# Six slots instead of four for the token tiles of the cluster pass, half of them filled from ScalarE's queue

## What is computed

```python
xn = _layernorm(x, axis=-1)
x = x + attn(xn, w_attn, b_attn, w_proj, b_proj) + ffn(xn, weight, bias, centroids, assignments)
# ffn:
dots = softmax(x @ centroids.T / 0.1, axis=-1)      # 64 clusters
hits = dots > 0.01
query_sel = any(hits, axis=1)                       # per token
cluster_sel = any(hits, axis=0)                     # over ALL tokens
row_sel = cluster_sel[assignments]
out = where(query_sel[:, None] & row_sel[None, :], x @ weight.T + bias, 0)
```

## Time and profile before

| what | us |
|---|---|
| median of 2 timed runs (6993.18 and 7485.42) | 7239.3 |
| the profiled execution, its own time | 7027.4 |
| its span, slowest core (core 1) | 7025.5 |
| spans of the 8 cores | 6952.6 to 7025.5 |
| median span of cores 0 to 3, of cores 4 to 7 | 6993.9, 6974.2 |
| mean granted clock of PE, share of full speed | 0.805 to 0.813 |

### The profile page before, as it was taken

The page is one execution under the profiler, slowest core; times in us unless marked ns, Lnnn a source line. Parts: engine busy times, 40 slices in busy tenths (PEclk is TensorE's granted clock), DMA queues, the critical chain, the costliest instruction groups (busy, mean ns, idle before and its releaser), DMA issues.

```text
span 7025.5 us, 98369 instructions; the slowest of 8 cores (6952.6 to 7025.5 us)
## 1 busy us (share of the span) xinstructions
PE 4684.8 (67%) x20715; PEld 1983.1 (28%) x20715; DVE 1906.3 (27%) x5321; ACT 1679.0 (24%) x3524; POOL 1613.6 (23%) x3133
## 2 busy tenths in 40 slices
PE   2218888888888896666666566355555557777676
PEld 1103333333333332122112111122222223333222
DVE  4421111111111100333333343355333322222222
ACT  4320000000000000222222222133444422222222
POOL 0011111111111111333333333000000034444443
PEclk9999988999988987777777777566555578888888
DMA  3322333323222223443444344211111054443443
GB/s 130 116 90 81 76 80 78 79 78 78 76 79 78 77 68 108 139 137 117 133 139 137 120 130 136 87 46 46 46 46 45 30 155 125 126 124 121 122 124 116
DMA packets 708128, 688.40 MB, mean 98 GB/s; under 512 B 100321, under 2 KB 562145, under 8 KB 701409
## 3 DMA queue, kind: packets, MB, share of 16 engines
q1 hardware_dynamic: 631906, 480.68, 23.8%
q0 software_dynamic: 75648, 201.44, 8.7%
HBM read 606.22 MB, written 75.50 MB: 97 GB/s over the span
## 4 chain that ended last, share of the span: by engine, by line
PE 52%; DVE 12%; ACT 11%; DMA 11%; issue 8%; POOL 3%; SPq 1%; DVEq 1%; ACTq 1%; POOLq 0%
PE p2p L87 27%; PE f5b L87 7%; PE f5a L87 7%; PE qp L87 4%; DMA d3x<-xT_all 4%; ACT a4e L80 4%; DMA qw<-w_attn 3%; ACT p2o L80 3%; POOL d3q L80 2%; DVE statc L80 2%; PE a4po L87 2%; PE a4pt L87 2%; DVE d3r L80 1%; ACT f5t L80 1%; DVE a4o L80 1%
## 5 line engine op out<-in xcount | busy, mean ns | idle before, releaser
L87 PE MATMUL p2p<-xn_fm,p2b 128*128 128x512 bf16 x8192 | 1961.6, 406 | 253.0 <-POOL p2b L80 244.4
L87 PEld LDWEIGHTS p2p<-xn_fm,p2b 128*128 128x128 bf16 x8192 | 840.2, 103 | 1374.0 <-issue 609.7
L87 PE MATMUL f5a<-ofm,f5pb 128*128 128x512 bf16 x2048 | 659.2, 406 | 312.9 <-DVE f5pb L80 312.9
L80 DVE CAST p2b<-p2w 128x128 bf16<-128x128 f32 x1024 | 232.3, 227 | 1972.5 <-PE p2p L87 1700.2
L87 PE MATMUL f5b<-xno,f5fb 128*128 128x512 bf16 x2048 | 651.8, 402 | 94.1 <-DVE f5fb L80 94.1
L87 PE MATMUL qp<-xno,qb 128*128 128x512 bf16 x2048 | 513.9, 410 | 288.6 <-DVE qb L80 229.4
L80 ACT ACTIVATE p2o<-p2p,battn 128x512 bf16<-128x512 f32 x256 | 175.9, 687 | 2052.0 <-PE p2p L87 2034.0
L99 POOL DMA_DIRECT2D f5f<-ffn_wT x1024 | 546.0, 537 | 262.5 <-issue 159.9
L80 POOL CAST p2b<-p2w 128x128 bf16<-128x128 f32 x1024 | 300.8, 294 | 1328.6 <-PE p2p L87 1152.0
L87 PE MATMUL a4po<-a4a,a4e 128*128 128x129 bf16 x2304 | 331.1, 269 | 292.1 <-ACT a4e L80 278.7
L80 ACT ACTIVATE a4e<-a4t 128x128 bf16<-128x128 f32 (+3 forms) x616 | 257.2, 418 | 643.3 <-DVE a4t L80 575.1
(11 more groups left out here) (112 smaller groups left out, 3806.7 us busy)
## 6 DMA issues: line engine op xcount, KB each, us to landing
p2w<-w_attn SPq DMA_DIRECT2D x2048, 64.0 KB, 2.3
d3x<-xT_all SPq DMA_DIRECT2D x512, 256.0 KB, 3.2
f5f<-ffn_wT POOLq DMA_DIRECT2D x1024, 64.0 KB, 2.3
f5p<-w_proj SPq DMA_DIRECT2D x1024, 64.0 KB, 2.1
qw<-w_attn POOLq DMA_DIRECT2D x512, 64.0 KB, 2.4
qw<-w_attn SPq DMA_DIRECT2D x512, 64.0 KB, 2.2
p1x<-x_full SPq DMA_DIRECT2D x16, 1024.0 KB, 5.9
p1x<-x_full POOLq DMA_DIRECT2D x16, 1024.0 KB, 8.0
```

What stands on the lines that cost most here:

```text
L80: instr = getattr(self.e, method)(*args, **kw)
L87: return getattr(self.e, method)(*args, **kw)
```

## The change

Three things change, all in `p3_gen` and its buffers. There are six slots instead of four. Slots 0 to 2 are still filled from SP; slots 3 to 5 are filled by DMAs issued on ACT's queue, with three semaphores of their own (`acq`). The waits in front of a fill are the same as before, but those in front of a fill of slots 3 to 5 now stand on ACT's queue. Even slots (0, 2, 4) are squared by ACT, odd ones (1, 3, 5) by POOL.

```diff
+        acq = [Ch(es, nc, f"acq{i}") for i in range(3)]
...
-                        for s in range(4)]
+                        for s in range(6)]
...
-                                s = (tg * NKC + kc) % 4
+                                s = (tg * NKC + kc) % 6
                                 sqe = AC if s % 2 == 0 else PO
-                                SY.dma(dsq[s], xtt[s][:],
-                                       xT_all[kc * 128:(kc + 1) * 128,
-                                              tg * 512:(tg + 1) * 512],
-                                       waits=[(DV.ch, b_done3[s]), q_done3[s]])
+                                xqe, xch = ((SY, dsq[s]) if s < 3
+                                            else (AC, acq[s - 3]))
+                                xqe.dma(xch, xtt[s][:],
+                                        xT_all[kc * 128:(kc + 1) * 128,
+                                               tg * 512:(tg + 1) * 512],
+                                        waits=[(DV.ch, b_done3[s]),
+                                               q_done3[s]])
                                 b_done3[s] = DV.op(
                                     "tensor_copy", xbb[s][:], xtt[s][:],
-                                    waits=[(dsq[s], dsq[s].n),
+                                    waits=[(xch, xch.n),
                                            (PE.ch, x_done[s])])
```

More of the change, by code:

```diff
@@ L472, in p3_gen @@
                     def p3_gen():
-                        x_done = [0, 0, 0, 0]
-                        b_done3 = [0, 0, 0, 0]
+                        x_done = [0] * 6
+                        b_done3 = [0] * 6
                         q_done3 = [(AC.ch, 0), (PO.ch, 0), (AC.ch, 0),
-                                   (PO.ch, 0)]
+                                   (PO.ch, 0), (AC.ch, 0), (PO.ch, 0)]
                         psd_free_ac = [0, 0]
```

## The result

The change made the kernel slower by 1.6%: the ratio to the kernel before is 1.0158, with a 95% interval of 1.0138 to 1.0177. The mean span of the 8 cores in the profiled execution went from 6982.8 to 7089.3 us, that of the slowest core from 7025.5 to 7100.7.

A forecast was written before the change was run, and what follows sets the result against it. The prediction took a loop of POOL square, SP refill and landing, 4.8 us per 4 steps, to bound the steps. Sixteen groups at 7.5 us more gave +119 us on 7027.4, so 7146 us; range 7050 to 7225.

The forecast's parts named there:

- Sum: Whole kernel: the profiled execution's 7027.4 us plus 119 us gives 7146 us, +1.7%.
- the surroundings: Whole kernel: outcomes around the forecast, +75 to +140 us; chance 0.45.
- Fills on ACT's queue: Group steps: square 4 waits for fill 4, delaying fill 5 and later refills; 1.31 us a step against 1.2 before.
- The steps of a group: Window from the end of `qo`, 32 steps: mean 46.2 us, 7.5 more than 38.7.
- The loop over two rounds: Group steps: chain from fill 4 through ACT, POOL and SP back to fill 4, 15.75 us for 12 steps.
- Square 4, 0.63 and 0.12 to the issue of fill 5: ACT's queue in the two-round loop: square 4 takes 0.63 us, then 0.12 until fill 5 is issued.
- Squares 5 and 1 on POOL, 2.8: POOL in the two-round loop: two squares of 1.3 us, 0.1 behind each, before SP's fill 1.
- The loop explains them: Kernel before, group steps: eight rounds of fill and square, 4.8 us per 4 steps, give 38.4 us for 38.7.
- Cost of a fill on ACT: ACT's issue time: taken as SP's 0.33 us; POOL's 0.54 would add up to 1.5 us a group.
- The Q projection and the tail keep their length.: Block windows outside the group steps: unchanged, as their queues hold the same instructions.
- The extra depth wins: Rival, group steps: the 4.8 us loop yields 6 steps, 32 steps take 27 us, total 6843 us; chance 0.04.
- The landing: Fill time: the trace's median 3.2 us kept over the skill's 2.6, by which the total would be about +23 us.

The follow-up runs named there:

- e3: Changed kernel with fills of odd slots (1, 3, 5, squared by POOL) issued by ACT and of even slots by SP; ratio 1.0058 to the kernel before.
- e4: Changed kernel with one edit: ACT squares slots 0 to 2, POOL slots 3 to 5; ratio 1.0099 to the kernel before.
- e8: Changed kernel with ACT's fills of slots 3 to 5 each written four steps earlier in the program; ratio 0.9832 to the kernel before.
- e10: e9 with all squares on ACT; ratio 0.9653 to the kernel before.
- e7: Kernel before, four slots filled by SP, with all squares on ACT; ratio 0.9972 to the kernel before.
- e5: Eight slots instead of the changed kernel's six, all filled by SP; ratio 0.9808 to the kernel before.
- e9: e5 with seven fills of a group written at the end of the group before, ahead of the weight fills; ratio 0.9726 to the kernel before.

## Why the prediction was right, and where it was not

- **The base, which failed.** Two steps of the prediction failed, the base of its "Sum" and, further down, the place of the cost on ACT's queue. The sum stands on the one profiled execution, 7027.4 us, and gives 7146. Set beside 7239.3, the time that the table ahead gives for the kernel before, this reads as a gain of 1.3%, while the kernel became 1.58% slower. The ten executions measured beside the changed kernel had a median of 7001.6 us, so the 7027.4 was 0.4% high as well, and that is most of the 0.6% by which 7146 lies above 7102, the median of the times after. A forecast of a small difference should state its ratio and its sign beside the time. Taken as a difference it came out: +119 us, +1.7%, against +1.58%, in the surroundings that had a chance of 0.45.
- **The mechanism, too narrow.** In "Fills on ACT's queue" the cost came from square 4, which waits for the fill issued just ahead of it. That wait is real (3.30 us in ACT's timeline). But e3 and e4 took it away and kept 42.0 and 43.9 us, 3 to 5 us above the kernel before. What the runs showed in its place is the general form: a fill on ACT goes out no earlier than the square written ahead of it, and so has no lead, whichever engine squares what it brings. The same fills written four steps ahead took the steps from 46.2 to 32.7 us (e8).
- **The steps of a group.** 46.2 forecast, 46.2 measured, which is better than its parts deserve, and in part luck. By start slot 0, 2 and 4 I had 44.95, 45.6 and 48.3; the means are 45.7, 46.6 and 46.6. At slot 4 the first fill leaves ACT 0.67 us before the end of `qo`, while the last `qo` is still running, where I had 0.1 behind it; that is about half of the miss there.
- **The loop over two rounds**, 15.75 us. In the group shown, fills of slot 4 leave 16.9 and 32.4 us after the end of `qo`: 15.5; over all groups and cores the median is 16.35. A step takes 1.34 us from the eighth on, for 1.31 in the sum. But terms of the sum were off and cancelled. "Square 4, 0.63 and 0.12 to the issue of fill 5" is 0.12, as a fill waits only for the start of the square ahead (3263.69, 3263.81), and the 0.63 of square 2 falls out in the same way (3259.75, 3259.88). "Squares 5 and 1 on POOL, 2.8" is the wrong path: it should be DVE's casts of slots 5, 0, 1 and 2, 4.1 us from 3236.61 to SP's issue at 3240.72 and 3.4 in the next round (3251.68 to 3255.10); SP's waits say the same (525.7 us for casts, 13.4 for POOL), and the chain holds 3.7 us of POOL squares a group, for 9.3 in the kernel before. And landings on this chain ran from 2.6 to 4.5 where I had 3.4 and 3.6; over all groups the medians are 3.3 for fill 4 and 3.1 for fill 5, and 4.2 for SP's fill of slot 2.
- **The cast beside POOL.** The forecast had no price for it. A cast that starts while a POOL square is running can take up to 1.31 us in the changed kernel, and takes 1.07 to 1.09 in the chain above. All of the 1275 casts, of 4096 on the 8 cores of the kernel before, that take over 0.9 us start inside a POOL square; in e10, with no POOL square, the longest of 512 is 0.48. A cast that starts just ahead of a POOL square keeps its 0.43, and then the square takes 1.30 instead of 1.04, as here in the timeline of the kernel before:

```profile
3442.58 0.43 DVE L80 CAST d3b<-d3x 128x512 bf16<-128x512 f32 x1 [1.00 <-PE d3pd L87]
3442.61 1.30 POOL L80 TENSOR_TENSOR d3q<-d3x 128x512 bf16<-128x512 f32 x1 [2.38 <-PE d3pd L87]
```

- **The kernel before.** "The loop explains them" was an agreement of sums: its chain holds 6.1 fills a group and 4.3 us of matmuls, not eight rounds of fill and square, and e7 missed by it.
- **Cost of a fill on ACT.** Taken as SP's 0.33: 0.334. POOL's 0.54 as an upper bound was not needed.
- **"The Q projection and the tail keep their length."** The tail did, 20.8. Q lost 0.6 us a block, since SP fetches three tiles early instead of four: 9 us given back. The term was missing, and the other edits show that it can be over 3 us a block (42.0 in e5, 38.8 in e9).
- **"The extra depth wins"**, 27 us: it was right about depth (e5 29.0) and rightly given little chance for this program, where fills on ACT can't run ahead.
- **The landing.** The Trainium skill (DMA: Bandwidth & Descriptors, Anatomy of one DMA) gives, for DMAs of GpSimd, a fixed cost plus a share by bytes, 2.6 us for this tile as an estimate. The minimum here, with fills from SP and ACT, is 2.5, the median 3.2 before and 3.4 after, and with more slots 4.0 to 5.1: in a stage with several tiles in flight its value lies at the minimum, and the prediction was right to keep the trace's.

## What to carry to other kernels

A load issued from an engine that also computes on the loaded tiles is only as early as its place in that engine's program. Slots give depth only if the fill is written ahead as well; with fills moved by four steps, six slots on the same queue went from 1.6% slower to 1.7% faster, and the steps from 46.2 us to 32.7, for 31.8 with all fills on SP. Other leads were not tried. A queue with nothing else on it, such as SP here, runs ahead by itself, but then what it fetches early competes with what runs at that time, and that has a price to look up in the stage before.

## What the runs showed that I had not expected

- A DMA on ACT's queue goes out about 0.13 us after the start of the ACT instruction ahead of it, if it waits for nothing else (3259.75 and 3259.88), and does not wait for that instruction's end.
- The shorter the steps, the higher PE's clock: the mean granted clock in them was 0.69 after, 0.73 before, 0.87 with six slots on SP and 0.93 in e10, though PE did the same matmuls. How much of each gain is this was not measured apart; the median first matmul of a step is 603 ns before and 377 in e10:

```profile
L87 PE MATMUL d3pd<-d3b,centbf x512: 376/377/638, 2799.2 to 4130.8; 128*64 128x512 bf16 x171
```

- Landings lengthen with depth, from a median of 3.2 us at four slots to 4.0 at six, 4.3 at eight, and 5.1 in e10 (slowest cores), whose steps move 299 GB/s. Whether fewer bytes or another layout of `xT_all` would shorten the steps further was not tried.
